# Transformer block kernel: other places for the work on weight pieces in the second pair, gates scaled on GpSimd

## The chip, the cores and the metric

One core of a Trainium2 chip. The metric is the device time of one execution in microseconds, median of several executions. Engines are TensorE (PE), VectorE (DVE), ScalarE (ACT), GpSimd (POOL) and the DMA queues, most of which SyncE (SP) issues.

## The reference

```
def attn(p, k_v):                       # p: LayerNorm(x), (4, 512, 512); k_v: ctx, (4, 512, 128)
    kv = k_v @ W_k.T + b_k
    out = einsum('bij,bjd->bid', p, kv)
    sim = einsum('bid,bjd->bij', out, kv) * 512 ** -0.5
    sim = layernorm(sim) * ln_gamma + ln_beta
    return softmax(sim)
def ffn(x):                             # 8 experts, D = F = 512, low rank terms in experts 0 and 1
    w = router_weights(x, Wr, temperature)          # (b, t, 8)
    gate, up = x @ Wg[e] (+ x @ Ga[e] @ Gb[e]), x @ Wu[e] (+ x @ Ua[e] @ Ub[e])
    mid = silu(gate) * up
    out = mid @ Wd[e] (+ mid @ Da[e] @ Db[e])
    return sum over e of w[..., e] * out
x = x + attn(layernorm(x), ctx)
x = x + ffn(layernorm(x))
```

All is in float32. 4 batches of 512 tokens.

## The kernel before

Each float32 matmul is made of three passes on high and low parts (hi x hi, lo x hi, hi x lo): `piece_hi` and `piece_lo` are such parts of weights, `xT_hi`, `tx_hi`, `mids_hi`, `mix_hi` and their `_lo` of activations. ScalarE makes a high part by a copy (rounding), VectorE the low part by a subtraction.

The first expert is computed in the usual way, mixed with the attention. The seven others are computed for two batches at a time: 14 steps k, 0 to 6 for batches 0 and 1 (the first pair) and 7 to 13 for batches 2 and 3 (the second pair). A matrix product of a step is done by a scheme of seven block products (as Strassen's, in Winograd's form): a **quad** is the seven products of one half m of gate, up or down, in the order 1, 5, (the fourth of the quad before), 6, 3, 2, 7; each is 6 matmuls of 128x512. Gate and up quads are `quad(j)`, j = 4k for gate 0, 4k+1 gate 1, 4k+2 up 0, 4k+3 up 1. In the first pair the down products are plain (`down_half`). In the second pair the down products are quads as well (`down_quad(d)`), and one step later: step k runs gate 0, gate 1, the two down quads of step k-1, up 0, up 1. The last step ends with a plain down product of its own (`down_half`), for which the transposed sums `acc_t` of the down quads are turned back by TensorE (`turn_back`) and added by VectorE (`add_turned_back`).

Per quad, ScalarE copies p1 (L968), p5 (L973) and u2 (L978) between the products; VectorE combines (`combine`: C12 at L1447, C22 at L1451), and the four results C12, C11, C22, C21 become gates by Silu on ScalarE (L990, L987, L984) or are multiplied with the gates into `mids` (`make_mid`, L1463 to L1470). Product 7 waits for the copy of u2, the fourth product for C22.

A weight **piece** (half of a matrix) has three slots. SP loads it when the fourth product of the piece three before is done; VectorE makes four sums of 128x256 (`piece_sums`, L1410 to L1415), ScalarE all seven high parts at once (`piece_high_part`, L955, 128x1792), VectorE the low parts in two operations (`piece_low_part`, L1422, 128x1024 and 128x768). The quad's first product waits for these.

As the down products of the second pair are added up over all steps before they are turned back, the gates are multiplied by the routing weights (`rw_rows`, loaded per step by DMA): `scale_gates(k, m)` (L1513), two operations of 128x1024 per half, the first when C12 and C11 are made, the second when C22 and C21 are; on VectorE. `make_mid` waits for it, and SP's next load of `rw_rows`. Per step k of 8 to 12 there are two such calls. GpSimd in the second pair issues three pairs of loads and clears `acc_t` (a memset from 643.56 for 3.52 us in the profile), no more.

All order is written out by hand: each engine's program is a list of such calls, and semaphores join them. In the first part of the kernel GpSimd makes low parts of the mids and of the first weights (L687, L697, L703). In the down part, ScalarE copies q1, q5 and u2 of a down quad (L1010, L1016, L1022), VectorE adds them and the results in PSUM to `acc_t` (L1547). The activation side of the down quads are sums of mids (`mix_of`) with high and low parts of their own (`operand_low_part`, L1540).

Of the kernel before, what the change touches and what calls it, by code (L numbers as in the profile page):

```python
# [74 lines left out]
def xattn_ffn_kernel(nc, x, xT, ctxT, wkT, bk, gamma, beta, wg, wu, wd, loraT, lora, wr, temperature, out):  # L75
# [6 lines left out]
    with ExitStack() as ctx:  # L82
# [687 lines left out]


        @block.scalar
        def _(act):
# [257 lines left out]
            def operands_of_first(k):  # L1031
# [9 lines left out]
                copy_u2(j + 3)  # L1041
                operand_high_part(k, 0, B21)
# [95 lines left out]
            for k in range(SWAP + 1, STEPS):  # L1138
# [3 lines left out]
                operand_high_part(k - 1, 1, B11)  # L1142
                if last:
                    piece_high_part(NUMBER[k, GATE, 1])
                copy_p5(j)
# [12 lines left out]
                gate_silu(k, 0, C21)  # L1158
                copy_u2(j + 1)
                piece_high_part(NUMBER[k - 1, DOWN, 0])  # L1160
# [4 lines left out]
                copy_q5(d)  # L1165
                gate_silu(k, 1, C21)
                copy_q_u2(d)
                piece_high_part(NUMBER[k - 1, DOWN, 1])
# [3 lines left out]
                if last:  # L1172
                    piece_high_part(NUMBER[k, UP, 0])
# [3 lines left out]
                if last:  # L1177
# [4 lines left out]
                    copy_p1(j + 3)  # L1182
                    mid_high_part(k, 0, C22)
                    copy_p5(j + 3)
                    copy_u2(j + 3)
                    for c in (C21,):
                        mid_high_part(k, 0, c)
                    for c in (C12, C11, C22, C21):
                        mid_high_part(k, 1, c)
                else:  # L1190
                    if k == STEPS - 2:
                        piece_high_part(NUMBER[k + 1, GATE, 0])
# [4 lines left out]
        def _(dve):  # L1197
# [309 lines left out]
            def scale_gates(k, m):  # L1507

                dve.wait_ge(rw_rows_loaded, 32 * (k - SWAP + 1))
                for pair in range(2):  # L1510
                    dve.wait_ge(gates_made, 8 * k + 4 * m + 2 * pair + 2)
                    two = gates[m][:, 2 * pair:2 * pair + 2, :]
                    nc.vector.tensor_tensor(two, two, rw_rows[:, :, :], ALU.mult).then_inc(gates_scaled, 1)  # L1513

# [34 lines left out]
            def add_u2_and_p5(d):  # L1549
# [6 lines left out]
                add_to_turned(d, C22, down_p5[:, :])  # L1556
                dve.wait_ge(q_copied, q_copy(6, d))
# [150 lines left out]
            def operands_of_first(k):  # L1708
# [3 lines left out]
                if k == STEPS - 2:  # L1712
                    piece_low_part(NUMBER[k + 1, GATE, 0])
# [4 lines left out]
                operand_low_part(k, 0, B11)  # L1718
                mix_of(k, 0, T2)
# [8 lines left out]
                operand_low_part(k, 0, T3)  # L1728
                operand_low_part(k, 0, B21)
                operand_low_part(k, 0, T4)  # L1730

            for k in range(SWAP + 1):
# [8 lines left out]
                if k == SWAP:  # L1741
# [22 lines left out]
                    scale_gates(k, 0)  # L1764
                    scale_gates(k, 1)
# [70 lines left out]
            for k in range(SWAP + 1, STEPS):  # L1836
# [9 lines left out]
                if last:  # L1846
                    piece_low_part(NUMBER[k, GATE, 1])
                mix_of(k - 1, 1, T2)
# [3 lines left out]
                make_mid(k - 1, 1, C21)  # L1852
# [7 lines left out]
                piece_sums(NUMBER[k - 1, DOWN, 0])  # L1860
                combine(k, GATE, 1, C12)
                piece_low_part(NUMBER[k - 1, DOWN, 0])
                combine(k, GATE, 1, C22)
                if not last:
                    scale_gates(k, 0)
                piece_sums(NUMBER[k - 1, DOWN, 1])
                add_u2_and_p5(d)
                add_c12(d)
                piece_low_part(NUMBER[k - 1, DOWN, 1])
                add_c11(d)  # L1870
                add_c22(d)
                if last:
                    piece_sums(NUMBER[k, UP, 0])
                else:
                    scale_gates(k, 1)
                add_c21(d)
                add_u2_and_p5(d + 1)
                if last:
                    piece_low_part(NUMBER[k, UP, 0])
                add_c12(d + 1)  # L1880
# [5 lines left out]
                if last:  # L1886
# [10 lines left out]
                    make_mid(k, 0, C21)  # L1897
                    combine(k, UP, 1, C12)
                    make_mid(k, 1, C12)
                    mid_low_part(k, 0, C21)  # L1900
                    wd_low_part(k)
                    combine(k, UP, 1, C22)
                    add_turned_back(1)
# [7 lines left out]
                else:  # L1911
                    if k == STEPS - 2:
                        piece_sums(NUMBER[k + 1, GATE, 0])
# [6 lines left out]
        def _(pe):  # L1920
# [188 lines left out]
            def quad(j, pending, down_pending=None):  # L2109
# [39 lines left out]
                if j == 4 * STEPS - 1:  # L2149
                    turn_back(1)  # L2150
# [190 lines left out]
```

## Time and profile before

| | |
|---|---|
| median of 3 runs | 1058.14 us (1057.99 to 1058.88) |
| the profiled execution's own time | 1058.47 us |
| its span, first to last instruction | 1056.7 us |
| PE busy | 1035.1 us, 98% |
| DVE busy | 764.8 us, 72% |
| ACT busy | 464.9 us, 44% |
| POOL busy | 76.1 us, 7%, nearly all in the first 200 us |
| chain that ended last | PE 77%, DVE 11%, ACT 4% |

The span leaves out 1.8 us around the program. Idle time of an engine is given in the rows with what ended it; matmuls overlap, so their starts tell more than their lengths. A row "x2" holds two instructions that stand together, and its time is from the start of the first to the end of the last.

### The profile page before, as it was taken

How to read it: one execution, taken by the hardware profiler on the slowest of the kernel's cores; microseconds unless marked ns; L12 is line 12 of the kernel's file. 1: busy time of each engine (PE TensorE's matmuls, PEld its weight loads, DVE VectorE, ACT ScalarE, POOL GpSimd, SP SyncE). 2: the span in 40 equal slices, each digit the busy share in tenths (PEclk: the TensorE clock that was granted, in tenths of full speed). 3: DMA queues.
4: the chain of work that ended last, by engine and by line, in shares of the span. 5: the costliest groups of instructions: out<-in, count | busy, mean ns of one | idle time of the engine just before them, and what ended most of it. 6: DMA issues, size and time to landing. Idle time of an engine off the chain costs nothing.

```text
span 1056.7 us, 12591 instructions
## 1 busy us (share of the span) xinstructions
PE 1035.1 (98%) x4641; PEld 841.7 (80%) x4641; DVE 764.8 (72%) x1292; ACT 464.9 (44%) x712; POOL 76.1 (7%) x105
## 2 busy tenths in 40 slices
PE   8999999999999999999999999999999999998998
PEld 5887787878888888888888888878787888886777
DVE  7878678877484856748487776868777686859684
ACT  4654363554443543444354343635345363525530
POOL 2511121100000010000000101000000000000000
PEclk9999999999999999999999999999999999999999
DMA  9410104339475574947534535445452644341222
GB/s 299 153 50 1 80 21 159 114 107 305 151 251 207 179 268 135 307 147 246 212 131 149 182 100 187 129 149 171 159 174 97 219 106 164 120 159 40 72 108 80
DMA packets 97629, 160.85 MB, mean 152 GB/s; under 512 B 5600, under 2 KB 66208, under 8 KB 96672
## 3 DMA queue, kind: packets, MB, share of 16 engines
q1 hardware_dynamic: 90656, 120.13, 35.1%
q0 software_dynamic: 6624, 39.85, 10.3%
q8 instruction: 37, 0.61, 0.2%
q14 instruction: 24, 0.20, 0.1%
q10 hardware_dynamic: 288, 0.07, 0.0%
HBM read 105.99 MB, written 54.03 MB: 151 GB/s over the span
## 4 chain that ended last, share of the span: by engine, by line
PE 77%; DVE 11%; ACT 4%; issue 3%; DMA 2%; POOL 0%; SPq 0%; DVEq 0%; ACTq 0%
PE gate_up L2039 13%; PE gate_up L2041 13%; PE gate_up L2040 13%; PE tiles L1925 6%; PE tiles L1927 6%; PE tiles L1926 6%; PE tiles L2057 3%; DVE piece_lo L1422 3%; PE tiles L2058 3%; PE tiles L2059 3%; ACT piece_hi L955 2%; PE gate_up L1996 2%; PE gate_up L1997 2%; PE gate_up L2002 2%; PE tiles L1961 1%
## 5 line engine op out<-in xcount | busy, mean ns | idle before, releaser
L2039 PE MATMUL gate_up<-xT_hi,piece_hi 128*128 128x512 f32 x448 | 175.4, 391 | 2.6 <-ACT p_sb L973 1.7
L2041 PE MATMUL gate_up<-xT_lo,piece_hi 128*128 128x512 f32 x448 | 174.4, 389 | 0.0
L2040 PE MATMUL gate_up<-xT_hi,piece_lo 128*128 128x512 f32 x448 | 174.3, 389 | 0.0
L2039 PE MATMUL gate_up<-tx_hi,piece_hi 128*128 128x512 f32 x336 | 131.2, 391 | 3.1 <-DVE mids L1451 2.5
L2040 PE MATMUL gate_up<-tx_hi,piece_lo 128*128 128x512 f32 x336 | 130.8, 389 | 0.0
L2041 PE MATMUL gate_up<-tx_lo,piece_hi 128*128 128x512 f32 x336 | 130.7, 389 | 0.0
L1422 DVE TENSOR_TENSOR piece_lo<-piece,piece_hi 128x1024 fp32r<-128x1024 f32 x96 | 101.5, 1099 | 19.5 <-ACT piece_hi L955 17.5
L968 ACT ACTIVATE gate_up<-gate_up 128x512 f32<-128x512 f32 x56 | 32.6, 582 | 181.4 <-PE gate_up L2041 122.3
L2039 PEld LDWEIGHTS gate_up<-xT_hi,piece_hi 128*128 128x128 f32 x448 | 84.1, 188 | 23.2 <-ACT p_sb L973 2.9
L1925 PE MATMUL tiles<-wd_hi,mids_hi 128*128 128x512 f32 x256 | 99.8, 390 | 2.0 <-DVE xacc L1588 1.5
L1927 PE MATMUL tiles<-wd_hi,mids_lo 128*128 128x512 f32 x256 | 99.6, 389 | 0.0
L1926 PE MATMUL tiles<-wd_lo,mids_hi 128*128 128x512 f32 x256 | 99.6, 389 | 0.0
L2041 PEld LDWEIGHTS gate_up<-xT_lo,piece_hi 128*128 128x128 f32 x448 | 84.1, 188 | 17.6
L2040 PEld LDWEIGHTS gate_up<-xT_hi,piece_lo 128*128 128x128 f32 x448 | 84.1, 188 | 17.0
L955 ACT ACTIVATE piece_hi<-piece 128x1792 fp32r<-128x1792 f32 x48 | 81.5, 1699 | 33.4 <-DVE piece L1415 33.4
L1478 DVE SCALAR_TENSOR_TENSOR xacc<-tiles,rw,xacc 128x512 f32<-128x512 f32 x64 | 44.3, 749 | 66.4 <-PE tiles L1927 66.4
L2039 PEld LDWEIGHTS gate_up<-tx_hi,piece_hi 128*128 128x128 f32 x336 | 63.0, 188 | 17.8 <-DVE mids L1451 3.3
L2041 PEld LDWEIGHTS gate_up<-tx_lo,piece_hi 128*128 128x128 f32 x336 | 63.1, 188 | 13.2
L2040 PEld LDWEIGHTS gate_up<-tx_hi,piece_lo 128*128 128x128 f32 x336 | 63.1, 188 | 13.0
L995 ACT ACTIVATE mids_hi<-mids 128x512 fp32r<-128x512 f32 x64 | 40.2, 629 | 58.5 <-DVE mids L1463 27.2
L1925 PEld LDWEIGHTS tiles<-wd_hi,mids_hi 128*128 128x128 f32 x256 | 48.1, 188 | 12.7 <-issue 1.9
L1996 PE MATMUL gate_up<-xT_hi,w_hi 128*128 128x512 f32 (+1 forms) x160 | 55.1, 360 | 1.6 <-POOL w_lo L697 0.8
(214 smaller groups left out, 1899.5 us busy)
## 6 DMA issues: line engine op xcount, KB each, us to landing
piece_spill<-piece_hi POOLq DMA_DIRECT2D x20, 896.0 KB, 4.4
piece_spill<-piece_lo POOLq DMA_DIRECT2D x20, 896.0 KB, 6.5
piece_hi<-piece_spill SPq DMA_DIRECT2D x20, 896.0 KB, 4.5
piece_lo<-piece_spill SPq DMA_DIRECT2D x20, 896.0 KB, 6.4
piece<-merged SPq DMA_DIRECT2D x28, 256.0 KB, 3.3
piece<-in_wg_dram SPq DMA_DIRECT2D x24, 256.0 KB, 4.3
piece<-in_wu_dram SPq DMA_DIRECT2D x24, 256.0 KB, 6.1
merged<-lora_w SPq DMA_DIRECT2D x6, 1024.0 KB, 6.1
```

What stands on the lines that cost most here:

```text
L955: nc.scalar.activation(piece_hi[n % 3][:, :, :], piece[n % 3][:, 1:8, :], ACT.Copy)\
L968: nc.scalar.activation(gate_up[:, BANK_C, :], gate_bank(j), ACT.Copy).then_inc(s1_made, 1)
L995: nc.scalar.activation(mids_hi[h][:, f, :], mids[h][:, f, :], ACT.Copy).then_inc(mids_hi_made, 1)
L1422: ins = nc.vector.tensor_tensor(piece_lo[j % 3][:, first:last, :], piece[j % 3][:, first:last, :], plain(piece_hi[j % 3][:, first - 1:last ...
L1478: nc.vector.scalar_tensor_tensor(tile_of(b, t), tiles[:, t, :], rw[:, (b * TT + t) * E + s:(b * TT + t) * E + s + 1], tile_of(b, t), ALU.m ...
L1925: nc.tensor.matmul(dst, w_h, x_h, start=first, stop=False)
L1926: nc.tensor.matmul(dst, w_h, x_l, start=False, stop=False)
L1927: return nc.tensor.matmul(dst, w_l, x_h, start=False, stop=last)
L1996: nc.tensor.matmul(dst, w_hi[:, m, k, cols], x_hi[:, k, tokens], start=(k == 0), stop=False)
L2039: nc.tensor.matmul(dst, w_h, x_h, start=first and kt == 0, stop=False, skip_group_check=True)
L2040: nc.tensor.matmul(dst, w_l, x_h, start=False, stop=False, skip_group_check=True)
L2041: ins = nc.tensor.matmul(dst, w_h, x_l, start=False, stop=last and kt == 1, skip_group_check=True)
```

## The change

In the second pair, the high part of a down piece is made on ScalarE ahead of the copy of u2 (piece 0) and ahead of gate C21 (piece 1), and its low part on VectorE ahead of the combinations of gate 1 (piece 0) and behind the first add only (piece 1). `scale_gates` goes from VectorE to GpSimd, with the same waits. In the last two steps parts of pieces and of `wd` are moved behind or ahead of copies and combinations, and TensorE turns the second half back ahead of product 3 of the last quad.

```diff
@@ block.gpsimd
             nc.gpsimd.memset(acc_t[:, :, :, :], 0.0).then_inc(late_made, 1)
+            def scale_gates(k, m):
+                pool.wait_ge(rw_rows_loaded, 32 * (k - SWAP + 1))
+                for pair in range(2):
+                    pool.wait_ge(gates_made, 8 * k + 4 * m + 2 * pair + 2)
+                    two = gates[m][:, 2 * pair:2 * pair + 2, :]
+                    nc.gpsimd.tensor_tensor(two, two, rw_rows[:, :, :], ALU.mult).then_inc(gates_scaled, 1)
+            for k in range(SWAP, STEPS - 1):
+                scale_gates(k, 0)
+                scale_gates(k, 1)
@@ block.scalar, operands_of_first
                 copy_u2(j + 3)
+                if k == STEPS - 2:
+                    piece_high_part(NUMBER[k + 1, GATE, 0])
                 operand_high_part(k, 0, B21)
@@ block.scalar, steps 8 to 13
                 operand_high_part(k - 1, 1, B11)
+                copy_p5(j)
                 if last:
                     piece_high_part(NUMBER[k, GATE, 1])
-                copy_p5(j)
...
                 gate_silu(k, 0, C21)
+                piece_high_part(NUMBER[k - 1, DOWN, 0])
                 copy_u2(j + 1)
-                piece_high_part(NUMBER[k - 1, DOWN, 0])
                 gate_silu(k, 1, C12)
...
                 copy_q5(d)
+                piece_high_part(NUMBER[k - 1, DOWN, 1])
                 gate_silu(k, 1, C21)
                 copy_q_u2(d)
-                piece_high_part(NUMBER[k - 1, DOWN, 1])
+                if last:
+                    piece_high_part(NUMBER[k, UP, 0])
                 copy_q1(d + 1)
                 copy_q5(d + 1)
                 copy_q_u2(d + 1)
-                if last:
-                    piece_high_part(NUMBER[k, UP, 0])
...
                     copy_p1(j + 3)
+                    copy_p5(j + 3)
                     mid_high_part(k, 0, C22)
-                    copy_p5(j + 3)
...
-                    if k == STEPS - 2:
-                        piece_high_part(NUMBER[k + 1, GATE, 0])
                     operands_of_first(k)
@@ block.vector, operands_of_first
                 make_mid(k, 0, C12)
-                if k == STEPS - 2:
-                    piece_low_part(NUMBER[k + 1, GATE, 0])
...
                 operand_low_part(k, 0, B11)
+                if k == STEPS - 2:
+                    piece_sums(NUMBER[k + 1, GATE, 0])
...
                 operand_low_part(k, 0, T3)
+                if k == STEPS - 2:
+                    piece_low_part(NUMBER[k + 1, GATE, 0])
@@ block.vector, step 7
-                    scale_gates(k, 0)
-                    scale_gates(k, 1)
                     operands_of_first(k)
@@ block.vector, steps 8 to 13
                 if last:
                     piece_low_part(NUMBER[k, GATE, 1])
+                    make_mid(k - 1, 1, C21)
...
-                make_mid(k - 1, 1, C21)
+                if not last:
+                    make_mid(k - 1, 1, C21)
...
                 piece_sums(NUMBER[k - 1, DOWN, 0])
+                piece_low_part(NUMBER[k - 1, DOWN, 0])
                 combine(k, GATE, 1, C12)
-                piece_low_part(NUMBER[k - 1, DOWN, 0])
                 combine(k, GATE, 1, C22)
-                if not last:
-                    scale_gates(k, 0)
                 piece_sums(NUMBER[k - 1, DOWN, 1])
-                add_u2_and_p5(d)
+                add_p5(d)
+                piece_low_part(NUMBER[k - 1, DOWN, 1])
+                add_u2(d)
                 add_c12(d)
-                piece_low_part(NUMBER[k - 1, DOWN, 1])
+                if last:
+                    piece_sums(NUMBER[k, UP, 0])
                 add_c11(d)
                 add_c22(d)
-                if last:
-                    piece_sums(NUMBER[k, UP, 0])
-                else:
-                    scale_gates(k, 1)
                 add_c21(d)
-                add_u2_and_p5(d + 1)
                 if last:
                     piece_low_part(NUMBER[k, UP, 0])
+                add_p5(d + 1)
+                add_u2(d + 1)
...
                     make_mid(k, 0, C21)
+                    wd_low_part(k)
+                    add_turned_back(1)
                     combine(k, UP, 1, C12)
...
-                    wd_low_part(k)
                     combine(k, UP, 1, C22)
-                    add_turned_back(1)
...
-                    if k == STEPS - 2:
-                        piece_sums(NUMBER[k + 1, GATE, 0])
@@ block.tensor, quad
                 product(j, 6, gate_bank(j))
+                if j == 4 * STEPS - 1:
+                    turn_back(1)
                 pe.wait_ge(p5_made, j + 1)
...
-                if j == 4 * STEPS - 1:
-                    turn_back(1)
```

VectorE in a step of 8 to 12, before: from the sums of the first down piece (`piece_88`) to the scaling of gate 1 (`gates_106`).

```order
L1410 TENSOR_TENSOR piece_88<-piece_88 128x256
L1411 TENSOR_TENSOR piece_88<-piece_88 128x256
L1413 TENSOR_TENSOR piece_88<-piece_88 128x256
L1415 TENSOR_TENSOR piece_88<-piece_88 128x256
L1447 TENSOR_TENSOR gates_106<-u_sb,gate_up 128x512
L1422 TENSOR_TENSOR piece_lo_91<-piece_88,piece_hi_94 128x1024
L1422 TENSOR_TENSOR piece_lo_91<-piece_88,piece_hi_94 128x768
L1451 TENSOR_TENSOR gates_106<-p_sb,gate_up 128x512
L1513 TENSOR_TENSOR gates_105<-gates_105,rw_rows 128x1024 x2
```

And the same stretch after the change (lines are those of the changed file).

```order
L1421 TENSOR_TENSOR piece_88<-piece_88 128x256
L1422 TENSOR_TENSOR piece_88<-piece_88 128x256
L1424 TENSOR_TENSOR piece_88<-piece_88 128x256
L1426 TENSOR_TENSOR piece_88<-piece_88 128x256
L1433 TENSOR_TENSOR piece_lo_91<-piece_88,piece_hi_94 128x1024
L1433 TENSOR_TENSOR piece_lo_91<-piece_88,piece_hi_94 128x768
L1458 TENSOR_TENSOR gates_106<-u_sb,gate_up 128x512
L1462 TENSOR_TENSOR gates_106<-p_sb,gate_up 128x512
```

The low parts of the piece have moved ahead of the combination of gate 1, and the scaling is gone. The next place is ScalarE in the same step, before: gate C21 of gate 0, then the copy of u2 and the high part.

```order
L973 ACTIVATE p_sb<-gate_up 128x512
L984 ACTIVATE gates_105<-gate_up 128x512
L978 ACTIVATE u_sb<-gate_up 128x2x256
L955 ACTIVATE piece_hi_94<-piece_88 128x1792
L990 ACTIVATE gates_106<-gates_106 128x512
```

After the change:

```order
L985 ACTIVATE p_sb<-gate_up 128x512
L996 ACTIVATE gates_105<-gate_up 128x512
L967 ACTIVATE piece_hi_94<-piece_88 128x1792
L990 ACTIVATE u_sb<-gate_up 128x2x256
L1002 ACTIVATE gates_106<-gates_106 128x512
```

The high part and the copy of u2 have changed places. GpSimd at the end of its program, after the change (the memset was its last instruction before):

```order
L769 MEMSET acc_t 128x4096
L777 TENSOR_TENSOR gates_105<-gates_105,rw_rows 128x1024 x2
L777 TENSOR_TENSOR gates_106<-gates_106,rw_rows 128x1024 x2
```

The last two rows repeat once for each of steps 7 to 12.

## Rows read from the trace of the kernel before

**Rows 1.** Profile page, part 1: busy time, share and instructions of the engines.

```profile
PE 1035.1 (98%) x4641; PEld 841.7 (80%) x4641; DVE 764.8 (72%) x1292; ACT 464.9 (44%) x712; POOL 76.1 (7%) x105
```

**Rows 2.** Waits of TensorE, second half: us in total, times, longest.

```profile
PE tiles L2057 <- DVE piece_lo L1422: 3.9, 12, 0.3
...
PE gate_up L2039 <- DVE piece_lo L1422: 0.3, 1, 0.3
```

**Rows 3.** Time line of TensorE, steps 11 and 12: start, us, instruction, idle before.

```profile
860.45 0.39 PE L2039 MATMUL gate_up<-xT_hi,piece_hi 128*128 128x512 f32 x1
...
861.58 0.39 PE L2041 MATMUL gate_up<-xT_lo,piece_hi 128*128 128x512 f32 x1
862.30 0.50 PE L2057 MATMUL tiles<-mids_hi,piece_hi 128*128 128x512 f32 x1 [0.33 <-DVE piece_lo L1422]
...
872.48 0.50 PE L2057 MATMUL tiles<-mids_hi,piece_hi 128*128 128x512 f32 x1 [0.33 <-DVE piece_lo L1422]
...
920.74 0.50 PE L2057 MATMUL tiles<-mids_hi,piece_hi 128*128 128x512 f32 x1 [0.32 <-DVE piece_lo L1422]
```

**Rows 4.** Time line of VectorE, steps 7 (first row) and 11.

```profile
650.46 4.63 DVE L1513 TENSOR_TENSOR gates<-gates,rw_rows 128x1024 f32<-128x1024 f32 x4 [0.87 <-DMA rw_rows<-rw_spill]
...
854.22 0.68 DVE L1540 TENSOR_TENSOR mids_lo<-mids,mids_hi 128x512 fp32r<-128x512 f32 x1
...
855.42 0.42 DVE L1410 TENSOR_TENSOR piece<-piece 128x256 f32<-128x256 f32 x1
...
856.55 0.42 DVE L1415 TENSOR_TENSOR piece<-piece 128x256 f32<-128x256 f32 x1
859.36 0.69 DVE L1447 TENSOR_TENSOR gates<-u_sb,gate_up 128x512 f32<-128x512 f32 x1 [2.39 <-PE gate_up L2041]
860.15 2.09 DVE L1422 TENSOR_TENSOR piece_lo<-piece,piece_hi 128x1024 fp32r<-128x1024 f32 x2
```

**Rows 5.** Time line of ScalarE, step 11.

```profile
853.59 0.58 ACT L987 ACTIVATE gates<-gate_up 128x512 f32<-128x512 f32 x1
...
856.57 0.60 ACT L984 ACTIVATE gates<-gate_up 128x512 f32<-128x512 f32 x1 [0.70 <-PE gate_up L2041]
857.93 0.60 ACT L978 ACTIVATE u_sb<-gate_up 128x512 f32<-128x512 f32 x1 [0.76 <-PE gate_up L2041]
858.42 1.69 ACT L955 ACTIVATE piece_hi<-piece 128x1792 fp32r<-128x1792 f32 x1
```

**Rows 6.** Groups of instructions of GpSimd, by form: busy us, mean ns, idle before.

```profile
L687 POOL TENSOR_TENSOR mid_lo<-mid,mid_hi 128x512 fp32r<-128x512 f32 x12 | 18.0, 1499 | 94.7 <-ACT mid_hi L808 94.7
...
L687 POOL TENSOR_TENSOR mid_lo<-mid,mid_hi 128x256 fp32r<-128x256 f32 x8 | 6.3, 788 | 6.4 <-ACT mid_hi L808 6.4
...
L703 POOL TENSOR_TENSOR w_lo<-first_raw_all,w_hi 128x512 fp32r<-128x512 f32 x4 | 5.0, 1272 | 1.1 <-ACT w_hi L794 1.1
```

**Rows 7.** Time line of VectorE, end of the first expert.

```profile
185.78 1.22 DVE L1483 TENSOR_TENSOR tx_sum<-tx_sum 128x1024 f32<-128x1024 f32 x1
186.91 1.53 DVE L1410 TENSOR_TENSOR piece<-piece 128x256 f32<-128x256 f32 x1
...
193.56 3.18 DVE L1422 TENSOR_TENSOR piece_lo<-piece,piece_hi 128x1024 fp32r<-128x1024 f32 x2
```

**Rows 8.** Time line of GpSimd, same stretch.

```profile
186.60 1.56 POOL L687 TENSOR_TENSOR mid_lo<-mid,mid_hi 128x512 fp32r<-128x512 f32 x1 [7.26 <-ACT mid_hi L808]
```

**Rows 9.** Time line of VectorE, steps 12 and 13.

```profile
948.55 0.42 DVE L1410 TENSOR_TENSOR piece<-piece 128x256 f32<-128x256 f32 x1 [2.96 <-DMA piece<-merged]
...
976.64 0.68 DVE L1451 TENSOR_TENSOR gates<-p_sb,gate_up 128x512 f32<-128x512 f32 x1
```

**Rows 10.** Time line of TensorE, step 13.

```profile
969.60 0.50 PE L2039 MATMUL gate_up<-xT_hi,piece_hi 128*128 128x512 f32 x1 [1.24 <-ACT p_sb L973]
...
1022.37 0.50 PE L2039 MATMUL gate_up<-xT_hi,piece_hi 128*128 128x512 f32 x1 [0.19 <-ACT p_sb L973]
...
1030.05 0.47 PE L1925 MATMUL tiles<-wd_hi,mids_hi 128*128 128x512 f32 x1 [1.54 <-DVE xacc L1588]
```

More of the change, by code:

```diff
@@ L1182, in _ @@
                     copy_p1(j + 3)
+                    copy_p5(j + 3)
                     mid_high_part(k, 0, C22)
-                    copy_p5(j + 3)
                     copy_u2(j + 3)
-                    for c in (C21,):
-                        mid_high_part(k, 0, c)
+                    mid_high_part(k, 0, C21)
                     for c in (C12, C11, C22, C21):
@@ L1505, in mid_low_part @@
                   .then_inc(mids_lo_made, 1)
[L1507 to L1513, printed above, removed]
             def mix_of(k, kt, o):
@@ L1547, in add_to_turned, with add_p5 @@
                 nc.vector.tensor_tensor(to, to, source, ALU.add).then_inc(q_added, 1)
-            def add_u2_and_p5(d):
+            def add_p5(d):
                 if d < 2:
@@ L1556, in add_u2_and_p5, with add_u2 @@
                 add_to_turned(d, C22, down_p5[:, :])
+            def add_u2(d):
                 dve.wait_ge(q_copied, q_copy(6, d))
```

## The prediction

> **What bounds the kernel now.** I read the page's busy times first: TensorE works 1035.1 us of a span of 1056.7 [rows 1], so all a reordering can win is 21.6 us of gaps, while a loss has no such bound. Then the waits of TensorE in the second half [rows 2]: the commonest is that of the first product of a down quad (L2057) for `piece_lo`, 12 times. Then the time line of TensorE at step 11 [rows 3], which stands for steps 8 to 12: its first down quad starts at 862.30, that of step 12 at 920.74, 58.4 us later. Matmuls of a quad start 0.227 us apart (860.45 and 861.58 are five apart); the first of the down quad is due 0.227 after 861.58, at 861.81, and comes at 862.30, so 0.49 is lost. From there to the next down quad it is 10.18 us, 42 matmuls being 9.53, so 0.65 is lost. With the start-up that follows each wait I count 0.6 per down quad, 1.2 per step, 7 us in six steps.
>
> VectorE's time line [rows 4] shows why: it makes the sums of the piece by 856.97, then idles 2.39 us for the combination C12 (L1447), and only then writes `piece_lo`, which ends at 862.24. ScalarE [rows 5] copies u2 first (L978) and makes `piece_hi` after it (L955).
>
> **The change, part by part.** *Work put ahead.* Read alone, the new order is right: `piece_hi` could start once gate C21 is done (856.57 + 0.60 = 857.2), `piece_lo` would be ready by 861.0, before 861.81; u2 would be copied by 859.5 and product 7, its reader, starts at 860.45. Both gaps of a step would go.
>
> *Scaling on GpSimd.* VectorE loses 24 operations of 128x1024 at 4.63 / 4 = 1.16 us [rows 4], 4.6 us per step. They lay after both things that matter for the first down quad, so taking them away hastens nothing there; they did stand ahead of the second piece's sums. No row has this operation on GpSimd. The nearest [rows 6]: 512 columns in 1.27 us (L703) or 1.50 (L687, waits for ports in it), 256 in 0.79. Bounds: 1.5, as if 1024 cost no more than 512, and 3.0, twice that. The slope from 0.79 to 1.27 gives 1.27 + 2 x 0.48 = 2.23, twice 1.27 is 2.54; I take 2.35 us, nearer to the slope, of which some 0.12 is start-up and 2.2 are work. The Trainium skill, "GPSIMD Engine Reference", 3.1, has 4497 ns for 2048 columns; half of it, an estimate, is 2.25 us, and by it the sum would end some 1.5 us lower; no trace here goes beyond 512 columns. GpSimd has 9.4 us per step of this against VectorE's 4.6, and nothing else in its queue behind.
>
> *The price: VectorE stands still meanwhile.* The first expert's end shows it [rows 7, 8]. GpSimd is asked at 186.60 for an operation with both inputs in SBUF, during a VectorE operation of the same kind (185.78 to 187.00). GpSimd ends at 188.16, 1.16 after VectorE's. VectorE's next, a 256-column sum that was already issued at 186.91, takes 1.53 instead of 0.42: it starts when GpSimd has ended. Again at 193.56, two `piece_lo` take 3.18 instead of the 2.09 of [rows 4]. So GpSimd gets in between two queued VectorE operations, and VectorE is held for GpSimd's whole work. The Trainium skill, "SBUF — State Buffer", Who interferes with whom, says the same: a VectorE instruction with two SBUF inputs contends with a GpSimd one that reads SBUF, and the pair of ports goes to one for the whole instruction. The trace agrees, 1.1 us per hold at 512 columns; were the ports shared without holding, the sum would be rival one's.
>
> Here the operations held are low parts (L1540), sums (L1410 to L1415), `piece_lo` (L1422) and adds of `down_p5`, `down_u2`; those with one input in PSUM (L1447, L1451) run on.
>
> *First down quad of steps 8 to 12.* Gates C12 and C11 are ready at 853.59 + 0.58 = 854.2 [rows 5]. GpSimd's first scaling starts behind or ahead of the low part at 854.22; either way VectorE has done both remaining low parts only at 857.7. The second is asked for at 857.2, when C21 is ready, and gets in at 857.7, until 859.9. The sums take from there 1.46, to 861.4, not 856.97. `piece_hi` (1.70) ends at 863.1. Now its new place hurts: u2's copy stands behind it and ends at 863.65, where product 7 wanted it at 860.45. TensorE waits 3.2 us, runs product 7 (1.36 and start-up 0.1) to 865.1, and `piece_lo` (2.09) is ready at 865.25. The down quad starts at 865.3 instead of 862.30: **+3.0**.
>
> *Second down quad.* C12 is combined after `piece_lo`, to 865.9; two gates of 0.6 follow, so the third scaling is asked for at 867.1 and gets in among the second piece's sums at 867.4, until 869.65. Sums end at 869.95, `piece_hi` at 871.7, gate C21 behind it at 872.2. That asks for the fourth scaling, while the first half of `piece_lo` runs (871.8 to 872.9). GpSimd holds until 875.1, the second half (0.8) ends at 875.9, the quad starts at 876.0. It was 10.18 behind the first, it is now 10.7: **+0.5**.
>
> So +3.5 per step, 17.5 in five steps. Behind the down quads VectorE's next operations wait for TensorE again, so nothing is carried over.
>
> *Step 7.* All four scalings follow the landing of `rw_rows` at 650.4 and run to about 660, over the mixes of VectorE. Between 0 and one hold of 2.2; I take 0.5, as only the last two holds meet work (make_mid C12, C22) and these had some slack.
>
> *Last step (13).* Nothing is scaled. Its three waits for a piece (two down, and up 0's, the last line there, [rows 2]) go by the argument above: 3 x 0.6 = 1.8. The work on the pieces of gate 0 and gate 1 moves behind combinations. But VectorE works through from 948.55, when gate 0's piece has landed, to gate 0's combination C22 at 976.64 [rows 9], which TensorE waits for. In the new order it does C12's two operations before 948.55 and then idles until up 0's product 7 is there, so it wins nothing and loses nothing: 976.6 stays, and the waits in front of it, that of 1.24 at 969.60 [rows 10] among them, only merge: 0. At 1022.37 and 1030.05 the waits (0.19 and 1.54, with start-up about 0.5 and 1.8) go, as copy_p5 no longer stands behind a mid, and add_turned_back(1) is done before C12's combination. Sum **-4.1**; bounds 0 (another wait takes their place) to -8.4 (all that TensorE loses from 954 on, by the starts in its time line).
>
> *Queues.* SP's load of `rw_rows` waits for the scaling of the step before: done at 875.1 + now, 876 before, and the load behind it waits for the fourth product of up 1, far later: nothing. GpSimd's memset of acc_t stands ahead of the first scaling and is over at 647.1, before `rw_rows` lands: nothing. No DMA is added or moved.
>
> Sum on the profiled execution: 1058.47 + 17.5 + 0.5 - 4.1 = 1072.4; its time is 0.3 over the median of the runs, so **1072** against 1058.14.
>
> **Rivals.** *One: GpSimd costs VectorE nothing* (it waits until VectorE's queue is empty, or both read side by side). Then the sums end at 857.0, both gaps of each step go, and it is 1058.1 - 5 x 1.2 - 4.1 = 1048, faster. What decides is the end of the sums: u2's copy comes 2.2 after it, so product 7 waits once they end after 858.2. For it speaks that the reordering is right by itself; against it the 1.53 and the 3.18 of [rows 7]. *Two: the hold is real, but the second scaling comes in only behind the four sums.* They end at 859.2, u2 at 861.45, `piece_lo`, held by the scaling, at 863.5: +1.2, and +0.2 in the second quad; 5 x 1.4 + 0.5 - 4.1 = +3.4, 1061.5. Against it: in [rows 7, 8] GpSimd never waited for a second VectorE operation. *Three: moves and losses cancel* (short holds of 1.4 us, as if 1024 columns cost 1.5 us): sums near 859.8 with both holds, +1.4 and -0.3, total 1.1 x 5 + 0.5 - 4.1 = +1.9, about 1060, at the edge of no change. *Dearer holds:* with 3.0 us each, both in front of the sums add 1.3, and the second quad 0.6: 1.9 x 5, 1082.
>
> **How the numbers follow.** Forecast as worked out, with small differences of the hold (1066 to 1079): 0.70. Rival two 0.10, three 0.06, rival one 0.12, dearer 0.02. No change is within 0.2%, 2.1 us, about what a measurement of this kernel can tell. Slower: 0.70 + 0.10 + 0.02 and half of three, 0.85; same 0.03; faster 0.12. The range 1060 to 1079 holds forecast, rival two and most of three, and leaves out rival one.
>
> **What would show it.** GpSimd's scalings near 2.3 to 2.9 us each; sums of the first down piece of a step with 2 us of hold in a row of 0.42; TensorE waiting some 3 us at product 7 of gate 1 for u2, five times, not in step 13; 61.9 us from step to step instead of 58.4; no wait of 1.5 before the last down matmuls. It is wrong if the sums keep 1.5 us in all, or if steps last 57.2 us.

## The result, and the profile after

| | before | after |
|---|---|---|
| median, run in turn on one chip | 1058.51 us | 1077.24 us (1075.49 to 1078.64) |
| ratio, 95% interval | | 1.0176 (1.0159 to 1.0194) |
| profiled execution, its span | 1058.47, 1056.7 us | 1075.49, 1073.8 us |

The kernel is 1.8% slower. The forecast was 1072; the range of 1060 to 1079 holds the result.

The page after, its busy times, and of its groups GpSimd's scaling:

```profile
span 1073.8 us, 12591 instructions
PE 1040.3 (97%) x4641; PEld 845.9 (79%) x4641; DVE 781.8 (73%) x1268; ACT 464.3 (43%) x712; POOL 141.7 (13%) x129
...
L777 POOL TENSOR_TENSOR gates<-gates,rw_rows 128x1024 f32<-128x1024 f32 x24 | 65.5, 2737 | 237.5 <-ACT gates L999 219.7
```

GpSimd has taken over 24 operations, 65.5 us, and TensorE does the same 4641 matmuls as in [rows 1]. VectorE has lost 24 operations of 1.16 us, 28 us, and is nevertheless busy for 17 us longer: its other operations have become longer by 45 us together.

TensorE's waits in the second half (us in total, times, longest):

```profile
PE gate_up L2042 <- ACT u_sb L990: 15.4, 5, 3.4
PE gate_up L2042 <- DVE piece_lo L1433: 3.7, 1, 3.7
PE tiles L2060 <- DVE piece_lo L1433: 2.5, 3, 1.0
PE gate_up L2042 <- DVE gates L1458: 0.4, 1, 0.4
PE tiles L1928 <- DVE mids_lo L1515: 0.4, 1, 0.4
```

Of the twelve short waits of the down quads for `piece_lo` three are left, 0.5 to 1.0 us long, at the second down quads of steps 9 to 11. Five of 3.0 to 3.4 us are new, at a place that never waited before: product 7 of gate 1, for the copy of u2. The time line of step 11 shows how. GpSimd (start, length, and in brackets the idle time before it and what ended it):

```profile
866.80 5.65 POOL L777 TENSOR_TENSOR gates<-gates,rw_rows 128x1024 f32<-128x1024 f32 x2 [41.17 <-ACT gates L999]
879.61 2.57 POOL L777 TENSOR_TENSOR gates<-gates,rw_rows 128x1024 f32<-128x1024 f32 x1 [7.16 <-ACT gates L999]
884.75 2.95 POOL L777 TENSOR_TENSOR gates<-gates,rw_rows 128x1024 f32<-128x1024 f32 x1 [2.58 <-ACT gates L996]
```

VectorE in the same stretch:

```profile
866.70 0.68 DVE L1543 TENSOR_TENSOR mids_lo<-mids,mids_hi 128x512 fp32r<-128x512 f32 x1
867.31 2.89 DVE L1543 TENSOR_TENSOR mix_lo<-mix,mix_hi 128x512 fp32r<-128x512 f32 x1
870.12 2.61 DVE L1421 TENSOR_TENSOR piece<-piece 128x256 f32<-128x256 f32 x1
872.65 0.41 DVE L1422 TENSOR_TENSOR piece<-piece 128x256 f32<-128x256 f32 x1
...
873.44 0.42 DVE L1426 TENSOR_TENSOR piece<-piece 128x256 f32<-128x256 f32 x1
875.62 2.09 DVE L1433 TENSOR_TENSOR piece_lo<-piece,piece_hi 128x1024 fp32r<-128x1024 f32 x2 [1.76 <-ACT piece_hi L967]
...
879.95 2.51 DVE L1426 TENSOR_TENSOR piece<-piece 128x256 f32<-128x256 f32 x1
...
884.23 4.29 DVE L1433 TENSOR_TENSOR piece_lo<-piece,piece_hi 128x1024 fp32r<-128x1024 f32 x2 [1.17 <-ACT piece_hi L967]
```

Four scalings and four holds: a low part of 0.68 takes 2.89, a sum of 0.42 takes 2.61, another 2.51, a pair of 2.09 takes 4.29. Each hold is 2.1 to 2.2 us, and a held operation ends as soon as the scaling beside it is over: the sum at 870.12 + 2.61 = 872.73, 0.28 behind the second scaling's end at 866.80 + 5.65 = 872.45; that at 879.95 ends at 882.46, 0.28 behind 879.61 + 2.57. ScalarE and TensorE behind them:

```profile
873.89 1.70 ACT L967 ACTIVATE piece_hi<-piece 128x1792 fp32r<-128x1792 f32 x1 [4.23 <-DVE piece L1426]
875.50 0.58 ACT L990 ACTIVATE u_sb<-gate_up 128x512 f32<-128x512 f32 x1
```

```profile
876.13 0.50 PE L2042 MATMUL gate_up<-xT_hi,piece_hi 128*128 128x512 f32 x1 [3.02 <-ACT u_sb L990]
888.57 0.50 PE L2060 MATMUL tiles<-mids_hi,piece_hi 128*128 128x512 f32 x1 [0.98 <-DVE piece_lo L1433]
```

The sums end late, the high part after them, u2's copy after that, and product 7 waits 3.02.

**Where the time went, step by step.** Starts of the first down quad of steps 8 to 13 in TensorE's time line, before and after:

| step | 8 | 9 | 10 | 11 | 12 | 13 | end of span |
|---|---|---|---|---|---|---|---|
| before | 687.13 | 745.48 | 803.89 | 862.30 | 920.74 | 984.80 | 1056.7 |
| after | 690.80 | 753.69 | 815.70 | 877.77 | 940.03 | 1005.32 | 1073.8 |
| later by | 3.67 | 8.21 | 11.81 | 15.47 | 19.29 | 20.52 | 17.1 |

It is 3.6 to 4.5 us per step through step 12, 1.2 more up to step 13, and 3.4 given back in the last step.

**What the waits do to TensorE's clock.** The windows of four stretches of 3 us behind such waits, with one away from them (of each engine busy us and, in brackets, instructions; PEclk is the granted clock as a share of 2.4 GHz):

```profile
core 0: us, PE busy (x) PEld busy (x) DVE busy (x) ACT busy (x) POOL busy (x), PEclk, DMA share, GB/s
690.90:693.80 2.90, 2.90 (x9) 2.31 (x8) 2.87 (x6) 1.31 (x3) 1.36 (x1) 0.56 0.00 0
752.00:755.00 3.00, 3.00 (x9) 2.38 (x8) 2.37 (x5) 1.12 (x2) 0.33 (x1) 0.52 0.00 0
800.00:803.00 3.00, 3.00 (x15) 2.49 (x14) 2.97 (x6) 1.34 (x4) 0.00 (x0) 1.00 0.64 182
940.10:943.10 3.00, 3.00 (x10) 2.37 (x9) 2.97 (x6) 1.40 (x3) 1.46 (x1) 0.58 0.03 5
984.30:987.30 3.00, 3.00 (x9) 2.36 (x8) 2.97 (x8) 1.11 (x2) 0.00 (x0) 0.55 0.00 0
```

In four of the five TensorE runs at the lower level, 1.2 GHz, nearly throughout (0.52 to 0.58): 9 or 10 matmuls are counted in 3 us, and 15 at 800, where the clock is 1.00. It had stood for 3.0 to 3.7 us shortly ahead of each of the four, for u2 or, ahead of the last, for gate 0's piece in step 13. In the profiled execution 29 matmuls start 0.43 us apart and not 0.23, in four places (690, 752, 940 and 984 us); behind the waits of steps 10 and 11 none do. Each costs 0.2, some of which disappears, since the next down quad would have waited for `piece_lo` anyway. The other three executions list a mean clock of 0.987 to 0.990 against 0.994 of the profiled one, and are 1.7 to 3.2 us longer.

### The profile page after: what moved, and what is told of

Its sections match the earlier page's. It is cut to its first block, busy times and chain, and to the rows that moved or that the text cites. A ratio compares the mean times of both kernels' runs of the same rounds, so it can differ in the third digit from the quotient of the medians.

```text
span 1073.8 us, 12591 instructions
## 1 busy us (share of the span) xinstructions
PE 1040.3 (97%) x4641; PEld 845.9 (79%) x4641; DVE 781.8 (73%) x1268; ACT 464.3 (43%) x712; POOL 141.7 (13%) x129
## 3 DMA queue, kind: packets, MB, share of 16 engines
q0 software_dynamic: 6624, 39.85, 10.1%
## 4 chain that ended last, share of the span: by engine, by line
PE 67%; DVE 20%; issue 5%; ACT 3%; DMA 1%; POOL 0%; DVEq 0%; SPq 0%; ACTq 0%
PE gate_up L2042 10%; PE gate_up L2043 10%; PE gate_up L2044 10%; PE tiles L1928 6%; PE tiles L1930 6%; PE tiles L1929 6%; PE tiles L2060 3%; PE tiles L2061 3%; PE tiles L2062 3%; DVE mix_lo L1543 3%; PE gate_up L1999 2%; PE gate_up L2000 2%; PE gate_up L2005 2%; DVE piece_lo L1433 2%; DVE mids_lo L1543 2%
## 5 line engine op out<-in xcount | busy, mean ns | idle before, releaser
L1433 DVE TENSOR_TENSOR piece_lo<-piece,piece_hi 128x1024 fp32r<-128x1024 f32 x96 | 112.4, 1212 | 33.9 <-ACT piece_hi L967 33.1
L777 POOL TENSOR_TENSOR gates<-gates,rw_rows 128x1024 f32<-128x1024 f32 x24 | 65.5, 2737 | 237.5 <-ACT gates L999 219.7
L1007 ACT ACTIVATE mids_hi<-mids 128x512 fp32r<-128x512 f32 x64 | 40.2, 629 | 56.3 <-DVE mids L1474 27.4
L1550 DVE TENSOR_TENSOR acc_t<-acc_t,tiles 128x512 f32<-128x512 f32 x48 | 31.9, 685 | 38.9 <-PE tiles L2062 37.6
```

The lines of the kernel that those rows point to most:

```text
L777: nc.gpsimd.tensor_tensor(two, two, rw_rows[:, :, :], ALU.mult).then_inc(gates_scaled, 1)
L1007: nc.scalar.activation(mids_hi[h][:, f, :], mids[h][:, f, :], ACT.Copy).then_inc(mids_hi_made, 1)
L1433: ins = nc.vector.tensor_tensor(piece_lo[j % 3][:, first:last, :], piece[j % 3][:, first:last, :], plain(piece_hi[j % 3][:, first - 1:last ...
```

## The experiments

The theory: GpSimd's scaling holds VectorE, through its reads, while VectorE makes the sums that everything waits for, and the new order by itself is a gain. Rivals: the new order costs the time (u2 behind the high part, above all); or GpSimd's instructions cost by standing beside VectorE's at all, read or not.

**1. Scaling back on VectorE, at its old places; every other move kept.**

```diff
@@ block.gpsimd
-            def scale_gates(k, m):
...
-            for k in range(SWAP, STEPS - 1):
-                scale_gates(k, 0)
-                scale_gates(k, 1)
@@ block.vector
+            def scale_gates(k, m):
...
@@ step 7, ahead of operands_of_first
+                    scale_gates(k, 0)
+                    scale_gates(k, 1)
@@ steps 8 to 12, behind combine(k, GATE, 1, C22), and behind add_c22 of the first down quad
+                    scale_gates(k, 0)
...
+                    scale_gates(k, 1)
```

> The changed kernel, with scale_gates back on VectorE at its old places; all other moves stay. Theory (GpSimd's reads hold VectorE, and the reordering itself is good): no wait of 3.2 us at product 7 in steps 8 to 12, no wait for piece_lo at the down quads, steps of 57.2 to 57.3 us. 5 x 1.2 us less than before, and 2.8 us less in the last part, as the trace after the change shows there: 1049 to 1050 us. Rival (moving piece_high ahead of the copy of u2 and piece_lo ahead of the combinations is itself what costs): still near 1075 us, with the wait for u2.

Measured: 1048.72 us, ratio 0.9906 (0.9891 to 0.9920). From 640 us on TensorE waits twice:

```profile
PE gate_up L2045 <- DVE piece_lo L1422: 3.7, 1, 3.7
PE gate_up L2045 <- DVE gates L1447: 0.2, 1, 0.2
```

Both gaps of a step are gone (down quads 57.12 us apart, before 58.4). So the order alone wins 10 us and the scaling on GpSimd costs 28.5. The one wait left, gate 0's in step 13, has 12 matmuls at the half clock behind it.

**2. Only the scaling moved to GpSimd; all else as before.**

```diff
@@ block.gpsimd, behind the memset of acc_t
+            def scale_gates(k, m):
...
+            for k in range(SWAP, STEPS - 1):
+                scale_gates(k, 0)
+                scale_gates(k, 1)
@@ block.vector
-            def scale_gates(k, m):
...
-                    scale_gates(k, 0)
-                    scale_gates(k, 1)
...
-                    scale_gates(k, 0)
...
-                    scale_gates(k, 1)
```

> The kernel before, with scale_gates alone moved to GpSimd, no other move. Theory: the first two scalings hold the low parts and sums as after the change, so piece_lo of down piece 0 is ready at the same time whatever stands around it, and the first down quad of steps 8 to 12 starts 3.0 us later than before; product 7 has no wait, the down quad has one of some 3.5 us instead. Second down quad +0.6. 5 x 3.6 + 0.5: 1077 us, up to 1081 with the lower clock behind such waits. Rival (the scaling on GpSimd costs nothing, or only relieves VectorE): 1055 to 1058 us.

Measured: 1099.03 us, ratio 1.0381 (1.0366 to 1.0396), far past that. The wait is the down quads' for `piece_lo` again, but long:

```profile
PE tiles L2055 <- DVE piece_lo L1434: 33.9, 12, 5.9
```

In the time line the third scaling, too, now falls in front of the first down quad. VectorE, GpSimd and TensorE at step 11:

```profile
881.35 2.62 DVE L1422 TENSOR_TENSOR piece<-piece 128x256 f32<-128x256 f32 x1
...
885.01 0.68 DVE L1459 TENSOR_TENSOR gates<-u_sb,gate_up 128x512 f32<-128x512 f32 x1
886.86 4.26 DVE L1434 TENSOR_TENSOR piece_lo<-piece,piece_hi 128x1024 fp32r<-128x1024 f32 x2 [1.17 <-ACT piece_hi L967]
```

```profile
887.97 2.34 POOL L777 TENSOR_TENSOR gates<-gates,rw_rows 128x1024 f32<-128x1024 f32 x1 [4.29 <-ACT gates L999]
```

```profile
891.18 0.80 PE L2055 MATMUL tiles<-mids_hi,piece_hi 128*128 128x512 f32 x1 [5.49 <-DVE piece_lo L1434]
```

In the old order C12 of gate 1 is combined ahead of `piece_lo`, so its gates are ready, and the scaling asked for, while the low part is at work: 4.26 in place of 2.09. Behind these waits, 5.5 to 5.9 us long, some matmuls start at the half clock in every step (42 in all). Steps last 65.7 to 67.0 us. My expectation had carried the two holds of the changed order over to the old one. With the scaling on GpSimd the new order is thus worth 22 us, not 10 (1099.03 - 1077.24 against 1058.8 - 1048.7): it puts `piece_lo` ahead of the combination that calls GpSimd.

**3. As changed, but u2 copied ahead of the high part again.**

```diff
@@ block.scalar, steps 8 to 13
-                piece_high_part(NUMBER[k - 1, DOWN, 0])
                 copy_u2(j + 1)
+                piece_high_part(NUMBER[k - 1, DOWN, 0])
```

> The changed kernel, with the copy of u2 ahead of the high part of down piece 0 again on ScalarE. My prediction named that order as where it hurts. Theory of the hold: product 7 runs on time, but piece_lo is ready no earlier, so the wait of 3.2 us only moves to the first product of the down quad: 1076 to 1078 us, as the changed kernel. Rival (ScalarE's order is the cause): 5 x 3.1 us less, 1061 to 1062 us.

Measured: 1078.63 us, ratio 1.0187 (1.0172 to 1.0202), within the spread of the changed kernel. The wait has only moved:

```profile
PE tiles L2060 <- DVE piece_lo L1433: 17.2, 6, 3.6
```

u2's new place decides where TensorE stands, not for how long; the late sums do that. The rival that blames the order on ScalarE, at 1061 to 1062, falls. The two kernels are not alike in their clock, though: this profiled execution has 50 matmuls at the half clock where the changed kernel's has 29, some 4 us more, and is 2.9 us longer.

**4. As changed, but GpSimd writes and doesn't read:** four memsets of 128x512 in a scratch tile in place of each scaling, so the routing weights of steps 7 to 12 are left out.

```diff
@@ block.gpsimd, scale_gates
-                    nc.gpsimd.tensor_tensor(two, two, rw_rows[:, :, :], ALU.mult).then_inc(gates_scaled, 1)
+                    for part in range(4):
+                        ...
+                        nc.gpsimd.memset(scratch[:, :], 0.0).then_inc(scratched, 1)
+                    pool.wait_ge(scratched, done + 1)
+                    pool.sem_inc(gates_scaled, 1)
```

> The changed kernel, where GpSimd does four memsets of 128x512 to a scratch tile in place of each scaling, about as long (4 x 0.6 us) and at the same times, but without reading SBUF. The gates stay unscaled, which leaves the routing weights of six steps out of the second pair. Theory (it is the reading that holds VectorE): sums of 0.42 us each, no row of 2.6 us, no wait at product 7: 1049 to 1050 us. Rival A (any access of GpSimd holds VectorE, write or read): VectorE is held about 0.5 us four times per scaling, 1065 to 1077 us. Rival B (the waits come from late gates, not from ports): as the changed kernel, 1077 us.

Measured: 1048.61 us, ratio 0.9907 (0.9890 to 0.9924). GpSimd, then VectorE beside it:

```profile
850.09 2.28 POOL L783 MEMSET scratch<- 128x512 f32 x4 [41.65 <-ACT gates L1007]
853.03 2.28 POOL L783 MEMSET scratch<- 128x512 f32 x4 [0.66 <-ACT gates L1004]
```

```profile
850.62 0.69 DVE L1551 TENSOR_TENSOR mix_lo<-mix,mix_hi 128x512 fp32r<-128x512 f32 x1
851.22 0.42 DVE L1429 TENSOR_TENSOR piece<-piece 128x256 f32<-128x256 f32 x1
```

The same low part and sum take 0.69 and 0.42 beside memsets, where they took 2.89 and 2.61 beside scalings asked for at the same points. It is the reading (or what comes with it) that holds VectorE, not GpSimd's being at work or its writing. VectorE executes the same 1268 instructions in both: it is busy for 737.7 us here and for 781.8 in the changed kernel, so the holds come to 44 us, 1.8 per scaling. The Trainium skill, "SBUF — State Buffer", Who interferes with whom, says so: a VectorE instruction with both inputs in SBUF contends with a GpSimd one that reads SBUF, not with one that only writes it. The runs agree with that rule: 0.42 and 0.69 beside memsets, 2.61 and 2.89 beside scalings.

**5. As changed, but GpSimd scales only once `piece_lo` of down piece 1 is written** (steps 8 to 12).

```diff
@@ block.gpsimd
             for k in range(SWAP, STEPS - 1):
+                if k > SWAP:
+                    n = NUMBER[k - 1, DOWN, 1]
+                    pool.wait_ge(piece_ready[n % 3], raw_in_slot(n))
                 scale_gates(k, 0)
```

> The changed kernel, with GpSimd's four scalings of steps 8 to 12 begun only when the low part of down piece 1 is written, so that they lie over adds and idle time of VectorE. Theory (what costs is the work that a hold falls on, not GpSimd's time as such): the holds are still there, 4 x 2.2 us per step, but no wait at product 7 nor at a down quad: 1048 to 1051 us. Rival (GpSimd's 9.4 us per step delay mids or the next loads, or hold TensorE or DMAs): above 1055 us.

Measured: 1050.10 us, ratio 0.9922 (0.9908 to 0.9937). GpSimd's four scalings of a step, and a VectorE operation that they hold:

```profile
865.90 10.28 POOL L777 TENSOR_TENSOR gates<-gates,rw_rows 128x1024 f32<-128x1024 f32 x4 [46.81 <-DVE piece_lo L1436]
```

```profile
874.37 2.35 DVE L1553 TENSOR_TENSOR acc_t<-acc_t,down_u 128x512 f32<-128x512 f32 x1 [0.44 <-ACT down_u L1037]
```

The scalings are as many and nearly as long, 2.57 each, and TensorE waits nowhere for them; steps last 57.12 us, as in the first experiment. But the expectation had the mechanism only in part: it had four holds of 2.2 per step still there, and they are nearly gone. In the stretch of these four scalings two additions are longer than 0.69, by 0.25 and 1.66, 1.9 us in the step. VectorE is busy for 748.7 us in all, 11 over experiment 4, where the changed kernel has 44. Two additions to `acc_t` from PSUM (`tiles`), one input in SBUF each, ran beside the first scaling at their usual length:

```profile
866.52 1.29 DVE L1553 TENSOR_TENSOR acc_t<-acc_t,tiles 128x512 f32<-128x512 f32 x2
```

So what the later start does is to lay the scalings over operations with an input in PSUM and over idle time, where they hold VectorE little; the hold that is left falls on an addition that TensorE doesn't wait for. That a hold of the full 8.8 us per step would cost nothing there isn't shown. It still wins nothing over the first experiment: VectorE has time for the scaling itself.

**6. Half of it: gate 0 scaled on VectorE, gate 1 on GpSimd.**

```diff
@@ block.gpsimd
-            def scale_gates(k, m):
...
             for k in range(SWAP, STEPS - 1):
-                scale_gates(k, 0)
-                scale_gates(k, 1)
+                pool.wait_ge(gates_scaled, 4 * (k - SWAP) + 2)
+                for pair in range(2):
+                    pool.wait_ge(gates_made, 8 * k + 4 + 2 * pair + 2)
+                    two = gates[1][:, 2 * pair:2 * pair + 2, :]
...
@@ block.vector
+            def scale_gates(k, m):
...
@@ step 7, ahead of operands_of_first; steps 8 to 12, behind combine(k, GATE, 1, C22)
+                    scale_gates(k, 0)
```

GpSimd begins gate 1 only when VectorE has scaled gate 0. In step 11 that is at 872.28, 2.5 us after C12 and C11 of gate 1 became gates, so this run also moves the third scaling and isn't purely half of the holds.

> The changed kernel with gate 0 scaled on VectorE again and only gate 1 on GpSimd: half of the holds. Theory: nothing falls on the sums of down piece 0, so product 7 and the first down quad are on time; the two scalings of gate 1 fall on the sums and on piece_lo of down piece 1, behind 2.3 us of VectorE's own scaling, and the second down quad waits 2 to 4 us in each of five steps: 1059 to 1069 us. Rival (the cost goes with GpSimd's number of operations): half of 28 us, 1063 us, but then with a wait at product 7.

Measured: 1066.89 us, ratio 1.0080 (1.0065 to 1.0095). TensorE's waits in the down quads:

```profile
PE tiles L2068 <- DVE piece_lo L1429: 8.4, 5, 1.7
PE tiles L2068 <- ACT down_u L1030: 6.6, 5, 1.3
```

No wait is left at product 7 of gate 1: those come from gate 0's two scalings. Gate 1's two cost 1.7 us per step at the second down quad, and 1.3 at product 7 of the first, where the copy of its u2 stands behind the second high part, which I had not foreseen. The rival's 1063 lies in the same range as the theory; only the place of the waits tells them apart.

**7 and 8. The wait of 3.7 at gate 0 in step 13.** From the first experiment on: with the work on that piece as before, and with it yet sooner.

```diff
@@ (7): block.scalar and block.vector, operands_of_first
                 copy_u2(j + 3)
-                if k == STEPS - 2:
-                    piece_high_part(NUMBER[k + 1, GATE, 0])
...
                 make_mid(k, 0, C12)
+                if k == STEPS - 2:
+                    piece_low_part(NUMBER[k + 1, GATE, 0])
...
-                if k == STEPS - 2:
-                    piece_sums(NUMBER[k + 1, GATE, 0])
...
                 operand_low_part(k, 0, T3)
-                if k == STEPS - 2:
-                    piece_low_part(NUMBER[k + 1, GATE, 0])
@@ (7): ahead of operands_of_first(k), on ScalarE and on VectorE
+                    if k == STEPS - 2:
+                        piece_high_part(NUMBER[k + 1, GATE, 0])
...
+                    if k == STEPS - 2:
+                        piece_sums(NUMBER[k + 1, GATE, 0])
@@ (8): block.scalar and block.vector, operands_of_first
+                if k == STEPS - 2:
+                    piece_high_part(NUMBER[k + 1, GATE, 0])
+                    copy_u2(j + 3)
...
-                copy_u2(j + 3)
-                if k == STEPS - 2:
-                    piece_high_part(NUMBER[k + 1, GATE, 0])
+                if k != STEPS - 2:
+                    copy_u2(j + 3)
...
+                if k == STEPS - 2:
+                    piece_low_part(NUMBER[k + 1, GATE, 0])
...
                 operand_low_part(k, 0, T3)
-                if k == STEPS - 2:
-                    piece_low_part(NUMBER[k + 1, GATE, 0])
```

> Scaling on VectorE as in the second experiment's kernel with that part undone (e1), and besides the work on gate 0's piece of the last step where it stood before. In e1 that piece's low part makes TensorE wait 3.7 us at the first product, and 14 to 15 matmuls behind it start 0.43 us apart instead of 0.23. Theory (VectorE bounds this stretch either way, so only the lower clock behind the one long wait is won back, 1.2 to 2.8 us): 1046 to 1047.5 us. Rival (the move of gate 0's work was a gain): above 1049 us.

> e1, with the high and low parts of gate 0's piece of the last step made sooner (high part ahead of the mixes' high parts, low part ahead of theirs), so that gate 0's quad starts on time and the wait moves to the fourth product behind the combination C22. VectorE has the same work up to there. Theory: a wait of some 2.5 to 3 us instead of 3.7, in two parts, with no half clock behind: 1046 to 1047.5 us. Rival (any wait of about 3 us brings the lower clock): as e1, 1048.7 us.

Measured: 1047.55 us, ratio 0.9898 (0.9883 to 0.9913), and 1048.11 us, ratio 0.9905 (0.9888 to 0.9921). TensorE's waits from 640 us on, of (7), then of (8):

```profile
PE gate_up L2045 <- DVE mids L1451: 2.5, 2, 1.7
PE gate_up L2045 <- DVE gates L1447: 1.7, 1, 1.7
```

```profile
PE gate_up L2047 <- DVE mids L1453: 2.1, 1, 2.1
PE gate_up L2047 <- DVE gates L1449: 1.7, 1, 1.7
PE gate_up L2047 <- DVE mids L1465: 1.1, 1, 1.1
```

The waits sum to 4.2 and 4.9 us against 3.9 in the first experiment, and yet both medians are lower, by 1.2 and 0.6 us. The medians alone don't separate the three: in the turn of (7) and (8) the kernel before ran 0.5 faster as well (1058.27 against 1058.81), and the ratios, 0.9898, 0.9905 and 0.9906, have intervals that overlap. The traces do, for the stretch in question: from the first down quad of step 12 to that of step 13 it is 64.79 us in the first experiment, 62.75 in (7) and 63.36 in (8), and no matmul of (7) or (8) starts at the half clock where 12 do there, worth some 2.4 us. An execution of the first experiment's kernel that lists a clock of 1.000 took 1047.53, within the 1047.23 to 1047.78 of (7). So three short waits, none over 2.1, cost less in these profiled executions than one long one of almost the same sum; the half clock behind the long one is enough to account for it. (7) came out at the upper end of what I expected and (8) 0.6 above; (8)'s rival, that any wait of some 3 us brings the lower clock, was not tested, as no such wait was left. (7), the scaling on VectorE and gate 0's piece as before, has the lowest median: 1047.55, 1.0% under the kernel before and 2.7% under the changed one.

## Why the prediction was right, and where it was off

- **Scaling on GpSimd, 2.35 us.** Right: the shortest, which ran with little beside it, takes 2.34 in the second experiment; its time in the changed kernel, 2.74 on average, contains waiting for VectorE.
- **The hold of 2.2 us** from [rows 7, 8], scaled from 512 to 1024 columns. Right: 2.1 to 2.2 four times in step 11. That reads, or what comes with them, are its cause is shown (experiment 4). Also right is that operations with one input in PSUM run on: two took 1.29 beside a scaling (experiment 5).
- **First down quad, +3.0.** Right in its chain. Counted from gate C11's start, 866.08 where [rows 5] have 853.59, 12.49 later, the sums end at 873.86 (forecast 873.9), `piece_lo` is ready and the quad starts at 877.77 (forecast 865.3 + 12.5 = 877.8); the wait is 3.02 (forecast 3.2).
- **Second down quad, +0.5.** Right where the clock didn't fall between: 888.57 - 877.77 = 10.80 in step 11, where 10.7 was given.
- **"Now its new place hurts: u2's copy stands behind it".** Right as a place, wrong as a cause. With the copy in front (experiment 3) the time is the same. The sum did not rest on it: `piece_lo` at 865.25 sets the quad's start.
- **The work put ahead.** Right: alone it wins 10.1 us, and rival one's figure of 1048 is what experiments 1 and 4 gave, the cases in which GpSimd costs VectorE nothing.
- **Step 7, 0.5.** The first down quad of step 8 is 3.67 later where 0.5 + 3.0 were forecast. Of this, step 7 has some 0.35: TensorE's matmuls are 0.21 earlier than before at 652 us and 0.14 later at 685. The rest is the wait of 3.38 for u2 and what follows it.
- **Last step, -4.1.** The end came as forecast: -3.4 behind its first down quad, where 4.1 less that quad's 0.6 is 3.5. Its head did not. That the new order there "wins nothing and loses nothing" and the waits "only merge: 0" failed: they merged into one of 3.69 for gate 0's piece, with the half clock behind it. Experiment 7, with this piece's work in its old place, is 2.0 us shorter in that stretch than experiment 1. The wait of 1.5 ahead of the last down matmuls is gone, as forecast.
- **The term that was missing: TensorE's lower clock.** The sum took a wait for its length and "start-up 0.1". The total landed in the range although it had nothing for this. The profiled execution rose by 17.0 us (1075.49 - 1058.47), 3.1 over the 13.9 forecast: 1.6 of it between the first down quads of steps 8 and 12 (19.29 - 3.67 = 15.6 where 4 x 3.5 = 14 was forecast), 1.3 between those of steps 12 and 13 (1.23 where 0.5 - 0.6 was), 0.2 ahead of step 8. The half-clock matmuls lie in these stretches: 4.54 is lost from step 8 to 9, which holds most of two of the four places, but 3.66 from 10 to 11, which holds none, 0.16 from the forecast. The median lies 1.8 above the profiled execution, and with a lower listed clock; no trace of those executions shows where, so for that part the clock is the likely cause, not a shown one.

Among the rivals, the time of 1077.2 rules out two (1061.5) and three (1060), but it lies as near to the dearer holds (1082) as to the forecast (1072). The trace decides there: both of gate 0's scalings get in ahead of the sums' end, at 2.2 us each and not 3.0.

## What to carry to other kernels

Before giving VectorE's elementwise work to an idle GpSimd, find what VectorE has queued at the moment at which the work is asked for: where those operations read both inputs from SBUF, they stand still for longer than the work took before (2.2 us for 1.16 saved, here), and it counts in full if TensorE waits for one of them. If it must go there, tie its start to the end of the urgent work (experiment 5), not to its data alone, and choose a stretch in which VectorE idles or takes an input from PSUM: the same 24 scalings then held VectorE for 11 us and not 44. When summing waits on TensorE, count the clock too: behind single waits of 3.7 us here came 7 to 12 matmuls at the half clock, behind none of 2.1 or less.

## What was not expected of the hardware

- Waits of about 3 us were followed by the lower clock in some steps (8, 9 and 12) and not in others (10 and 11) of one execution, at nearly equal length; the one of 3.7 in step 13 was followed by it in every kernel that had it (7 to 12 matmuls), and in experiment 3 so were all five of 3.3 to 3.6. What separates the cases stays open.
- GpSimd's memsets of 128x512, four in 2.28 us, ran beside VectorE's two-input operations without lengthening them: 0.42 and 0.69, as alone.
- The same 24 scalings cost 40.2 us in the old order and 28.5 in the new one, so the new order is worth 21.8 us with them on GpSimd and 10.1 without.
